# A graph network of 12,500 nodes: the node layers in units of tiles inside the aggregation passes, with two tables and parts kept in DRAM

## The chip, the cores and the metric

The kernel runs on one core of a Trainium2 chip. The metric is device time in microseconds (us) of one execution. The work goes over five engines: PE (matmuls), DVE (vector), ACT (activations), POOL (here mostly the indirect DMAs that gather rows) and SP (plain DMAs).

## The reference

`x` is 12500 × 96, with 200,000 edges `src -> dst`, sorted by `dst`. Six of the seven graph layers are a sum over incoming edges of rows of a node array:

```python
h = relu(layernorm(x)); y = h
for i in range(2):                       # L0
    agg = segment_sum((y @ W0[i] + b0[i])[src], dst)
    y = concat([y @ W1[i] + b1[i], agg]) @ W2[i] + b2[i]
    y = y / std(y)
x = x + y
h = relu(layernorm(x))                   # L1: mean over the edges
x = x + segment_sum(h[src] @ W + b, dst) / max(deg, 1)[:, None]
h = relu(layernorm(x))                   # L2: three GCN layers with self loops
x = x + gcn(relu(gcn(relu(gcn(h))))) 
h = relu(layernorm(x))                   # L3: a small network per edge
e = relu(concat([h[src], h[dst]]) @ Wm1 + bm1) @ Wm2 + bm2
m = segment_sum(e * edge_attr, dst)
out = x + relu(concat([h, m]) @ Wu1 + bu1) @ Wu2 + bu2
```

## The kernel before, in words

Six **passes** (a = 0 to 5; one per sum), then the **edge network** of L3, and between them seven **node phases** (`in`, l0a, l0b, l1, l2a, l2b, l2c) and a last one (`fin`). A node phase turns the sums of a pass (AGG, turned: features on partitions) into the next rows `h`.

**A pass** does its sum in two ways at once. (1) POOL gathers: 88 groups of 8 indirect DMAs (`gather_tile`, L578), each 128 rows of 384 bytes from the DRAM `table` of `h`. PE multiplies them with one-hot matrices that DVE makes (L1167), in `window_sums` (L1522, 8 tiles a group); DVE adds the result to AGG (L1172). (2) Dense blocks: 55 blocks of 128 destinations, for which a count matrix `amat` (fp8, built in pass 0 by POOL's scatters, L593) is multiplied with all of `h` (`piece`, L1598: 100 matmuls of 288 columns a block, in AC = 5 pieces). `h` lies for this in SBUF in three bf16 parts (PARTS: high part, middle part, low part, 3 × 96 columns a tile). The three results of a block are summed (L1240), turned (L1605) and added to AGG (L1251). A pass is 11 **turns** (PE's `turn`, L1607) of 8 slots; a slot is one group of gathers and 5/8 of a block, in an order written out by hand. The flag `fast`, computed from the edges on the chip, chooses this way; else `all_groups` gathers everything.

**A node phase** (`node` on each engine: L1054, L1429, L721, L639) is a stage apart, in 10 chunks of 10 tiles of 125 rows: ACT copies the sums (L735), PE takes the product with the weights (`product`, L1475), DVE runs the chain of layernorm, std or relu (`chunk`, L1066 to L1145), PE turns `h` back to AGG's shape (`turned`, L1486; ACT evicts it, L773), ACT writes the high and middle parts (L762, L781), POOL the two subtractions between them (`split`, L657, L660) and SP stores `h` to `table` (`node_stores`, L390). l0a and l0b also rebuild a turned `h` from the parts (`unsplit`, L1439). `x` is kept in DRAM (`xres`). The next pass begins when all ten chunks are stored: POOL and PE wait for the last of n_st and n_lo:

```python
pool.wait_ge(n_st, 2 + (a + 1) * NCH)      # aggregation(a), POOL
pe.wait_ge(n_lo, 2 + (a + 1) * NCH)        # with_dense(a), PE
```

## Time and profile before

| | before |
|---|---|
| median of 3 runs | 10097.45 us (10087.99 to 10098.42) |
| the profiled execution | 10094.99 us, its span 10093.3 us |
| mean granted PE clock | 0.891 of full |
| PE, POOL busy | 7510.8 us (74%), 6698.0 us (66%) |
| DVE, ACT busy | 2912.4 us (29%), 831.6 us (8%) |

The span is the time between the first and the last instruction of the profiled execution. A share of busy time is an average over stages with different limits, so the stages have to be read one by one. On this time axis the stages are: loads and indices to 265 us, phase `in` to 374, pass 0 to 2434, then l0a, pass 1, l0b, pass 2 and so on; l2c ends at 7923, the edge network at 9885, and `fin` is the rest.

### The profile page before, as it was taken

The page shows a single profiled execution, that of the slowest core. Times are in us where ns is not written, and L with a number is a line of the kernel's source. Part 1 is how long each engine was busy: PE and PEld are TensorE (multiplying, and loading weights), DVE is VectorE, ACT ScalarE, POOL GpSimd, SP SyncE. Part 2 cuts the span into 40 slices and gives each one's busy share as a digit, 9 for nine tenths or more (in the row PEclk, how much of TensorE's full clock was granted, in tenths as well). Part 3 has the DMA queues.
Part 4 walks back from the last instruction along what each step waited for, and adds up shares of the span by engine and source line. Part 5 has one row for each costly group of instructions (what it writes and reads, how often), then busy time and mean ns, then how long its engine had stood idle before and what let it go on. Part 6 is the DMA issues. An engine that isn't in the chain of part 4 may idle for free.

```text
span 10093.3 us, 154577 instructions
## 1 busy us (share of the span) xinstructions
PE 7510.8 (74%) x55633; PEld 6121.5 (61%) x55633; DVE 2912.4 (29%) x5105; ACT 831.6 (8%) x1100; POOL 6698.0 (66%) x6862
## 2 busy tenths in 40 slices
PE   0155554446899869996999799979997677777777
PEld 0144443335777757775777677767776565666665
DVE  1533333331211241113111211121113344444441
ACT  0100000002100120003000200020002111111111
POOL 0577777774677547774777577757773577777771
PEclk9977777777899979996999799979996799999997
DMA  9333333322455435553555355535552344444442
GB/s 372 93 100 96 91 99 99 98 89 60 121 141 142 114 101 142 142 141 105 141 141 142 92 142 141 142 92 141 141 142 85 110 135 136 136 136 135 135 135 65
DMA packets 662964, 1264.24 MB, mean 125 GB/s; under 512 B 238941, under 2 KB 241535, under 8 KB 662757
## 3 DMA queue, kind: packets, MB, share of 16 engines
q1 hardware_dynamic: 409686, 862.57, 28.2%
q0 software_dynamic: 216992, 309.23, 14.2%
q10 hardware_dynamic: 36080, 90.12, 2.3%
q8 instruction: 78, 1.28, 0.1%
q14 instruction: 128, 1.05, 0.0%
HBM read 1112.96 MB, written 148.37 MB: 125 GB/s over the span
## 4 chain that ended last, share of the span: by engine, by line
POOL 61%; issue 21%; PE 7%; DVE 3%; DMA 2%; ACT 2%; SPq 2%; ACTq 0%; DVEq 0%; POOLq 0%
POOL G L578 53%; POOL amat L593 8%; PE PS L1475 2%; SPq L345 2%; PE PS L1598 2%; PE PS L1493 1%; ACT work L735 1%; DMA xres<-work 1%; PE PS L1486 1%; DVE small L1091 1%; PE PS L1439 1%; ACT work L750 0%; PE PS L1454 0%; PE PS L1522 0%; DVE work L1145 0%
## 5 line engine op out<-in xcount | busy, mean ns | idle before, releaser
L578 POOL DMA_INDIRECT G<-table,SRC x5792 | 5531.2, 955 | 1796.8 <-issue 1761.7
L1598 PE MATMUL PS<-PARTS,work 125*128 125x288 bf16 (+1 forms) x33000 | 4313.8, 290 | 729.3 <-DMA work<-amat 729.3
L1598 PEld LDWEIGHTS PS<-PARTS,work 125*128 125x128 fp8e4 x33000 | 3253.6, 99 | 1655.2 <-issue 743.6
L1522 PE MATMUL PS<-work,G 128*96 128x128 f32 (+1 forms) x8448 | 1091.2, 285 | 665.8 <-issue 410.3
L1522 PEld LDWEIGHTS PS<-work,G 128*96 128x96 f32 (+1 forms) x8448 | 1009.8, 172 | 755.4 <-issue 629.0
L1172 DVE TENSOR_TENSOR AGG<-AGG,PS 96x128 f32 (+1 forms) x724 | 206.0, 285 | 3173.5 <-PE PS L1522 2820.3
L593 POOL DMA_INDIRECT amat<-SVAL,ADDR x864 | 847.2, 981 | 274.5 <-issue 260.9
L1167 DVE TENSOR_TENSOR work<-PS,REL 128x1024 f32<-128x1024 f32 x724 | 878.4, 1214 | 49.3 <-POOL PARTS L660 25.1
L1536 PE MATMUL PS<-work,QW 128*96 128x512 f32 x784 | 426.3, 626 | 329.9 <-DMA G<-table,SRC 327.5
L1326 DVE TENSOR_TENSOR work<-work,PS 128x1024 f32<-128x1024 int32 x196 | 393.2, 2006 | 777.4 <-PE PS L1538 770.9
L1475 PE MATMUL PS<-W,work 97*125 97x96 f32 (+1 forms) x1800 | 389.8, 413 | 260.0 <-ACT work L735 129.2
L1233 DVE TENSOR_SCALAR_CACHE_REDUCE work<-work,KEYC 128x384 bf16<-128x384 f32 x864 | 528.2, 611 | 184.9 <-DVE work L1233 115.4
L1240 DVE TENSOR_REDUCE work<-PS 128x96 f32<-128x288 f32 x330 | 151.0, 458 | 1403.0 <-PE PS L1598 1402.9
L1475 PEld LDWEIGHTS PS<-W,work 97*125 97x125 f32 (+1 forms) x1800 | 373.9, 323 | 285.2 <-ACT work L735 139.6
L1538 PEld LDWEIGHTS PS<-ident,G 128*96 128x96 f32 x3136 | 397.8, 168 | 218.2 <-issue 218.2
L1554 PE MATMUL PS<-work 128*96 128x128 f32 x3136 | 383.9, 276 | 195.1 <-DVE work L1177 195.1
L735 ACT ACTIVATE work<-AGG 97x1250 f32 (+1 forms) x60 | 143.7, 2401 | 4476.1 <-DVE AGG L1251 4476.1
L1554 PEld LDWEIGHTS PS<-work 128*96 128x96 f32 x3136 | 347.4, 163 | 221.4 <-issue 221.3
L1538 PE MATMUL PS<-ident,G 128*96 128x128 f32 x3136 | 419.6, 278 | 0.0
L836 ACT ACTIVATE work<-PS,bcols 96x512 f32<-96x512 f32 x392 | 246.5, 677 | 1757.3 <-PE PS L1546 1711.1
L657 POOL TENSOR_TENSOR work<-work,PARTS 125x960 f32<-125x960 f32 x70 | 140.0, 2000 | 373.5 <-ACT PARTS L762 369.0
L1546 PE MATMUL PS<-W,work 97*128 97x96 f32 x3136 | 377.2, 273 | 0.5 <-DVE AGG L1172 0.5
(180 smaller groups left out, 2811.3 us busy)
## 6 DMA issues: line engine op xcount, KB each, us to landing
work<-amat SPq DMA_DIRECT2D x1650, 320.0 KB
work<-in_dst_dram SPq DMA_DIRECT2D x196, 512.0 KB, 5.1
G<-table,SRC POOLq DMA_INDIRECT x5792
amat<-work ACTq DMA_DIRECT2D x55, 1600.0 KB, 17.5
work<-in_edge_attr_dram SPq DMA_DIRECT2D x196, 384.0 KB
work<-keys SPq DMA_DIRECT2D x108, 640.0 KB, 6.3
table<-work SPq DMA_DIRECT2D x70, 468.8 KB
xres<-work SPq DMA_DIRECT2D x30, 468.8 KB
```

The costliest lines, as they stand in the source:

```text
L578: pool.indirect_dma_start(G[:, k, i, 0:D], None, table, bass.IndirectOffsetOnAxis(ap=SRC[:, tile:tile + 1], axis=0)).then_inc(done, 16)
L593: pool.indirect_dma_start(amat, bass.IndirectOffsetOnAxis(ap=ADDR[:, tile:tile + 1], axis=0), SVAL[:, tile:tile + 1], None).then_inc(s_sca ...
L1167: return dve.tensor_tensor(dst, places.unsqueeze(1).to_broadcast([P, TPG, WIN]), rel.unsqueeze(2).to_broadcast([P, TPG, WIN]), ALU.is_equal)
L1233: dve.tensor_scalar(JUNK, KB[k][:, n * P:(n + 3) * P], KEYC[:, bass.ds(tile, 1)], None, ALU.is_equal, ALU.add, accum_out=MULT[:, bass.ds(t ...
L1326: dve.tensor_tensor(OHT[k].rearrange("w (i p) -> w i p", i=TPG), DROW[k].rearrange("w (p i) -> w i p", i=TPG), ESTART[:, bass.ds(g, 1)].un ...
L1475: last = pe.matmul(o, stage[0:rows, j * NP:(j + 1) * NP], w, start=(m == 0), stop=(m == len(parts) - 1))
L1522: last = pe.matmul(PS[0:rows, k, 0:WIN], G[:, place, i, 0:rows], OH[k][:, i, :], start=(i == 0), stop=(i == TPG - 1))
L1536: pe.matmul(PS[0:D, bank, :], QW[:, q, :], OHT[k][:, b * HE:(b + 1) * HE], start=True, stop=False)
L1538: last = pe.matmul(PS[0:D, bank, i * P:(i + 1) * P], G[:, q, 4 * b + i, 0:D], ident[:, :], start=False, stop=(i == 3))
L1546: last = pe.matmul(PS[:, OUT_B[b], (i % 4) * D:(i % 4 + 1) * D], RT[:, i * P:(i + 1) * P], w_m2, start=True, stop=True)
L1554: last = pe.matmul(EWIN, MSG[:, i, :], OH[k][:, i, :], start=(i == 0), stop=(i == TPG - 1))
L1598: last = pe.matmul(PS[:, DENSE_B[b], 0:width], AB[m][0:NP, jj * WIN:(jj + 1) * WIN].bitcast(FP8), PARTS[0:NP, j * PW:j * PW + width], star ...
```

## The change

Nodes are laid out anew: 98 tiles of 128 rows (row = tile × 128 + p; 44 rows of padding) in place of 100 tiles of 125, so a dense block has 98 matmuls, in 7 pieces of 14. The phase after pass a now runs **inside pass a**, on the rows whose sums are complete: in 22 **units**, of 5 tiles (half 0: the dense rows) or 4 tiles (half 1: the gathered rows; the last has 3). Each turn from 1 to 10 carries two units in four steps of one slot each (half 0 from slot 0, half 1 from slot 4; in pass 0 from 2 and 5); the last two units follow the pass.

- The new rows go to the other one of two tables (`tables[k]`); the parts go to DRAM (`newparts`, stored by ACT) and SP loads them into PARTS at the end of the pass (`new_parts`): pieces 0, 1, 2, 4, 5 once the parts of all but the last two units are stored and the dense matmuls are done, pieces 3 and 6 after the last store.
- POOL has no node work left: the two subtractions of the split are DVE's (`rest` L1282, `third_part` L1289). Loads of `x` and stores of table, `x` and parts are issued by ACT.
- Node buffers are single and 5 tiles wide (H, XC, XL, HTS). PE's steps are the first of a slot's end: `product` (L1695) in step 0, `turned` (L1703) in step 2.
- The sum of a block is turned into its own bank (columns 384 to 511), at piece 3 (TURN_AT) instead of piece 1, and the next block in that bank waits for d_add, the add that reads it.
- The degrees are loaded with 12544 runs of 4 bytes (SP, `DEG[:, :]` in the diff), before block 1 of pass 1.
- `in` has 22 units; `fin` has 25 groups of up to 4 tiles, with the turned `h` loaded from DRAM (`hturned`), and buffers of 2.
- `fast` has two more conditions: the base of gather group 108 is at least 6400, and each of the last gathered rows of a turn is at least 7552.

```diff
-NP, NJ = 125, 100
-CH = 10
-PAIRS = NJ // CH // 2
+NT = 98
+NPAD = NT * 128
...
-AC = 5
-ACW = NJ // AC * WIN
+AC = 7
+ACW = NT // AC * WIN
...
+TURN_AT = 3
+HALVES, UNITS = 2, 2 * TURNS
+UNIT_AT = 4
+UT = 5
+SLOT_OF = ((0, UNIT_AT), (2, 5))
+PHASES = ("in", "l0a", "l0b", "l1", "l2a", "l2b", "l2c")
...
-        table = dram("table", (N, D))
+        tables = [dram(f"table{k}", (NPAD, D)) for k in range(2)]
+        hturned = dram("hturned", (D, NPAD))
+        newparts = nc.dram_tensor("newparts", (P, NT * PQ), BF16, kind="Internal").ap()
...
-        table_rows = table.rearrange("(p j) f -> p (j f)", j=NJ)
+        def tiles(half, u):
+            if half == 0:
+                return u * 5, 5, u * 2
+            return u * 4 + DB, 3 if isinstance(u, int) and u == TURNS - 1 else 4, u * 2 + 1
+        def rows_dram(ap, t0, n):
+            return ap[bass.ds(t0 * P, n * P), :].rearrange("(j p) f -> p j f", p=P)
...
+            def new_parts(a):
+                with sp.If(fast > 0):
+                    sp.wait_ge(d_mm, AC + a * DB * AC)
+                    sp.wait_ge(S["par"], prev16(S, "par", a, UNITS - 2))
+                    load_parts(a, (0, 1, 2, 4, 5))
+                    load_block(0, a * DB)
+                    if a < 3:
+                        sp.wait_ge(S["uns"], done(S, "uns", a))
+                    sp.wait_ge(S["par"], 16 * done(S, "par", a))
+                    load_parts(a, (3, 6))
...
+            for a in range(1, 6):
+                if a > 1:
+                    new_parts(a)
+                with sp.If(fast > 0):
+                    with sp.Fori(1, DB) as d:
+                        load_block(d, a * DB)
...
-                def split(c, k):
-                    if name == "fin":
-                        return
-                    parts = parts_of(c)
-                    pool.wait_ge(n_hi, c + (h0 + 1))
-                    pool.wait_ge(n_lo, c + (h0 + 2))
-                    pool.nop(nofuse=True)
-                    pool.tensor_tensor(c3(R1), c3(H[k]), parts[0], ALU.subtract).then_inc(n_r1, 1)
-                    pool.wait_ge(n_mid, c + (h0 + 1))
-                    pool.nop(nofuse=True)
-                    pool.tensor_tensor(parts[2], c3(R1), parts[1], ALU.subtract).then_inc(n_lo, 1)
...
+            def stage(s, phase, half, u):
+                t0, n, v = tiles(half, u)
+                act.wait_ge(s["out"], prev(s, "out", phase, v))
+                act.nop(nofuse=True)
+                act.activation(AGS[phase > 1][:, 0:n * P], AGG[:, bass.ds(t0 * P, n * P)], ACT.Copy).then_inc(s["ags"], 1)
...
+            def step(s, phase, q, half, u):
+                name = PHASES[phase]
+                if name in ("l0a", "l0b") and q == 0:
+                    copy_turned_parts(s, phase, half, u)
+                if q == 0:
+                    stage(s, phase, half, u)
...
+                if name != "l2c" and q == (2 if name == "l0b" else 1):
+                    store_rows(s, phase, half, u)
+                    first_part(s, phase, half, u)
+                if name != "l2c" and q == (3 if name == "l0b" else 2):
+                    second_part(s, phase, half, u)
+                if name in ("l1", "l2a", "l2b") and q == 2 or name == "l2c" and q == 1:
+                    evict(phase, half, u)
+                if name != "l2c" and q == (2 if name == "l0a" else 3):
+                    store_parts(s, phase, half, u)
...
+                if q == 3:
+                    next_x(phase, half, u)
...
+                            if start or not 0 <= q < 4:
+                                continue
+                            if q == 0 and half == 0:
+                                act.wait_ge(d_add, i * SIDE + (a * DB + 1))
+                            if q == 0 and half == 1:
+                                act.wait_ge(f_acc, i * SLOTS + (a * GG + UNIT_AT + 2))
+                            step(S, a + 1, q, half, i - 1)
...
+            def rest(s, phase, half, u):
+                t0, size, v = tiles(half, u)
+                dve.wait_ge(s["hi"], this(s, "hi", phase, v))
+                dve.tensor_tensor(u3(SQ if phase else RIN, size), u3(H, size), parts_of(phase, t0, size)[0],
+                                  ALU.subtract).then_inc(s["r1"], 1)
+            def third_part(s, phase, half, u):
+                t0, size, v = tiles(half, u)
+                parts = parts_of(phase, t0, size)
+                dve.wait_ge(s["mid"], this(s, "mid", phase, v))
+                dve.tensor_tensor(parts[2], u3(SQ if phase else RIN, size), parts[1], ALU.subtract).then_inc(s["lo"], 1)
...
-                def add_block(d, windows):
-                    block_cols = AGG[0:rows, bass.ds(d * WIN, WIN)]
-                    dve.wait_ge(d_turn, d + (b0 + 1))
-                    dve.wait_ge(f_acc, windows + (g0 + 2))
-                    dve.wait_ge(d_add, d + (b0 + 1))
-                    dve.tensor_tensor(block_cols, block_cols, PS[0:rows, 4, 0:WIN], ALU.add).then_inc(d_add, 1)
+                def add_block(d, b, windows):
+                    block_cols = AGG[0:rows, bass.ds(d * WIN, WIN)]
+                    dve.wait_ge(d_turn, d + (b0 + 1))
+                    dve.wait_ge(f_acc, windows + (g0 + 2))
+                    dve.wait_ge(d_add, d + (b0 + 1))
+                    dve.tensor_tensor(block_cols, block_cols, PS[0:rows, DENSE_B[b], 3 * P:4 * P], ALU.add).then_inc(d_add, 1)
...
+            def product(s, phase, half, u):
+                name = PHASES[phase]
+                t0, n, v = tiles(half, u)
+                sums = lambda j, rows: AGS[phase > 1][0:rows, j * P:(j + 1) * P]
+                if name in ("l0a", "l0b"):
+                    pe.wait_ge(s["hts"], this(s, "hts", phase, v))
...
+                for j in range(n):
+                    o = PS[:, 6, j * D:(j + 1) * D]
+                    if name in ("l0a", "l0b"):
+                        l = name == "l0b"
+                        pe.matmul(o, HTS[:, j * P:(j + 1) * P], w_self[l], start=True, stop=False)
+                        last = pe.matmul(o, sums(j, D + 1), w_nb[l], start=False, stop=True)
+                    elif name == "l1":
+                        last = pe.matmul(o, sums(j, D + 1), w_l1, start=True, stop=True)
+                    else:
+                        last = pe.matmul(o, sums(j, D), w_l2[("l2a", "l2b", "l2c").index(name)], start=True, stop=True)
+                last.then_inc(s["out"], 1)
...
+            def step(s, phase, q, after, half, u):
+                name = PHASES[phase]
+                if q == 0 and not after and name in ("l0a", "l0b"):
+                    unsplit(s, phase, half, u)
+                if q == 0 and after:
+                    product(s, phase, half, u)
+                if after and (q == 2 and name in ("l1", "l2a", "l2b") or q == 1 and name == "l2c"):
+                    turned(phase, half, u)
+                if after and q == 2 and name == "l2c":
+                    halves(half, u)
...
-                        pe.wait_ge(d_cp, d + (b0 - 1))
+                        pe.wait_ge(d_add, d + b0)
+                    if not first and isinstance(d, int) and d == 0:
+                        pe.wait_ge(p_ld[m], 16 * a)
...
-                def turn_sums(d, b):
-                    pe.wait_ge(d_cp, d + (b0 + 1))
-                    pe.wait_ge(d_add, d + (b0 + 1))
-                    pe.transpose(PS[0:rows, 4, 0:WIN], DSB[DENSE_T[b]][:, 0:rows], ident[:, :]).then_inc(d_turn, 1)
+                def turn_sums(d, b):
+                    pe.wait_ge(d_cp, d + (b0 + 1))
+                    pe.transpose(PS[0:rows, DENSE_B[b], 3 * P:4 * P], DSB[DENSE_T[b]][:, 0:rows], ident[:, :]).then_inc(d_turn, 1)
...
+                def turn(i, start=False):
+                    from_b = -off if start else 0
+                    for s in range(SLOTS):
+                        for half in range(HALVES):
+                            if not start and s == SLOT_OF[first][half]:
+                                step(S, a + 1, 0, False, half, i - 1)
+                        if first:
+                            gathered(i, s)
+                        for q in SHARE[s]:
+                            b, m = divmod(q, AC)
+                            d = i * SIDE + (b + off)
+                            if b < from_b:
+                                continue
+                            if m == TURN_AT and not (start and b == from_b):
+                                turn_sums(d - 1, (b - 1) % SIDE)
+                            piece(d, b, m)
+                        if not first:
+                            gathered(i, s)
+                        for half in range(HALVES):
+                            q = s - SLOT_OF[first][half]
+                            if start or not 0 <= q < 4:
+                                continue
+                            step(S, a + 1, q, True, half, i - 1)
...
```

**Place 1, PE, one turn of pass 3.** Before, in phase l2a, apart from the pass (L1475 the product, L1486 the turned `h`):

```order
L1475 MATMUL PS<-W,work 125x96 [waits n_read,n_ags]
L1475 MATMUL PS<-W,work 125x96 x9
L1481 REGISTER_ALU
L1482 REGISTER_ALU [waits n_h]
L1486 MATMUL PS<-ident,work 96x125 [waits n_ev]
L1486 MATMUL PS<-ident,work 96x125 x9
```

Now, in a turn of pass 3 (L1825 the dense pieces, L1831 the turned block sum, L1745 the sums of the gathered rows, L1695 the product of a unit of 5 tiles):

```order
L1831 MATMUL PS<-ident,work 96x128 [waits d_cp]
L1825 MATMUL PS<-PARTS,work 128x288 [waits d_ld3]
L1825 MATMUL PS<-PARTS,work 128x288 x13
L1810 ISA
L1811 ISA [waits f_oh]
L1745 MATMUL PS<-work,G 96x128 [waits f_acc,f_rows0]
L1745 MATMUL PS<-work,G 96x128 x7
L1681 ISA
L1682 REGISTER_ALU [waits n_read]
L1685 REGISTER_ALU [waits n_ev]
L1695 MATMUL PS<-W,work 128x96 [waits n_ags]
L1695 MATMUL PS<-W,work 128x96 x4
L1825 MATMUL PS<-PARTS,work 128x288 [waits d_ld4]
L1825 MATMUL PS<-PARTS,work 128x288 x13
```

The product of ten tiles stood between others of its kind; it is now one of five tiles between a window's sums and a dense piece, and everything behind it on PE stands if n_read, n_ev or n_ags comes late.

**Place 2, DVE, slot 1 of a turn of pass 3** (L1357 a one-hot, L1251 to L1274 the chain of the unit, L1439 the add of a block, L1362 the add of a window):

```order
L1251 TENSOR_TENSOR work<-PS,DINV 128x480
L1255 TENSOR_TENSOR work<-work,W 128x480 [waits n_read]
L1196 REGISTER_ALU
L1218 ISA [waits n_chain]
L1220 REGISTER_ALU [waits n_tab]
L1223 REGISTER_ALU [waits n_r1,n_hi]
L1274 SCALAR_TENSOR_TENSOR work<-work,DINV 128x480 [waits n_tr]
L1439 ISA [waits d_add,f_acc,d_turn]
L1439 TENSOR_TENSOR AGG<-AGG,PS 96x128
L356 ISA
L356 TENSOR_LOAD rowi
L1385 REGISTER_ALU
L1388 REGISTER_ALU [waits f_acc,f_sum]
```

The three instructions of 480 columns stood in the stage apart, ten times with 960 columns; L1439, the add whose d_add PE's next block in that bank waits for, stands right behind them.

**Place 3, PE, the end of a pass (l2a):** the two units that are left, of 5 and 3 tiles.

```order
L1695 MATMUL PS<-W,work 128x96 [waits n_ags,n_ev,n_read]
L1695 MATMUL PS<-W,work 128x96 x4
L1703 MATMUL PS<-ident,work 96x128 [waits n_read,n_h]
L1703 MATMUL PS<-ident,work 96x128 x4
L1695 MATMUL PS<-W,work 128x96 [waits n_ags,n_ev,n_read]
L1695 MATMUL PS<-W,work 128x96 x2
L1703 MATMUL PS<-ident,work 96x128 [waits n_read,n_h]
L1703 MATMUL PS<-ident,work 96x128 x2
```

Before, ten products and ten turned chunks stood here.

## Rows read from the trace of the kernel before

**Rows 1.** The page, the chain of work that ended last, by engine

```profile
POOL 61%; issue 21%; PE 7%; DVE 3%; DMA 2%; ACT 2%; SPq 2%; ACTq 0%; DVEq 0%; POOLq 0%
```

**Rows 2.** Windows: span, PE, PEld, DVE, ACT, POOL busy (x), PE clock, DMA, GB/s

```profile
265.00:374.00 109.00, 0.00 (x0) 0.00 (x0) 54.37 (x63) 41.99 (x47) 46.58 (x30) 1.00 0.32 88
374.00:2434.00 2060.00, 1033.64 (x6963) 804.27 (x6963) 700.51 (x2070) 22.54 (x108) 1538.75 (x1568) 0.75 0.31 95
...
3475.00:3700.00 225.00, 121.08 (x722) 116.81 (x723) 122.31 (x133) 102.25 (x110) 50.69 (x37) 0.55 0.24 73
...
4742.00:5633.00 891.00, 853.14 (x6963) 694.79 (x6963) 163.47 (x285) 0.00 (x0) 669.54 (x704) 0.99 0.53 140
5633.00:5745.00 112.00, 65.18 (x300) 60.43 (x300) 36.41 (x32) 62.69 (x59) 36.82 (x19) 0.56 0.13 42
...
7647.00:7923.00 276.00, 154.93 (x700) 145.66 (x700) 107.33 (x112) 91.95 (x90) 44.32 (x30) 0.51 0.22 70
7923.00:9885.00 1962.00, 1455.36 (x10057) 1177.27 (x10058) 846.59 (x971) 243.97 (x388) 1485.76 (x1562) 0.98 0.49 136
9885.00:10093.00 208.00, 165.85 (x756) 110.22 (x756) 18.69 (x21) 31.71 (x64) 11.08 (x16) 0.73 0.18 50
4850.00:5550.00 700.00, 672.57 (x5508) 548.18 (x5506) 128.20 (x224) 0.00 (x0) 530.27 (x558) 1.00 0.54 141
```

**Rows 3.** Groups by line, pass 3 (4742 to 5633 us): busy, mean ns, idle before

```profile
L1598 PE MATMUL PS<-PARTS,work 125*128 125x288 bf16 x5500 | 701.0, 286 | 13.0 <-DMA work<-amat 13.0
L578 POOL DMA_INDIRECT G<-table,SRC x704 | 669.5, 951 | 218.4 <-issue 214.2 <-SPq L394 4.1
```

**Rows 4.** PE's waits, inside pass 3 (4850 to 5550 us): total, times, longest

```profile
PE PS L1522 <- issue: 19.9, 26, 1.7
```

**Rows 5.** Timeline at the start of pass 3, POOL: start, us

```profile
4742.84 1.00 POOL L578 DMA_INDIRECT G<-table,SRC  x1 [4.15 <-SPq L394]
```

**Rows 6.** Timeline, end of pass 3 and the stage l2a

```profile
5625.66 0.95 POOL L578 DMA_INDIRECT G<-table,SRC  x1 [0.30 <-issue]
...
5633.10 0.28 DVE L1251 TENSOR_TENSOR AGG<-AGG,PS 96x128 f32<-96x128 f32 x1
...
5636.16 8.71 PE L1475 MATMUL PS<-W,work 96*125 96x96 f32 x40 [3.45 <-ACT work L735]
...
5642.38 1.16 DVE L1133 TENSOR_TENSOR work<-work,W 125x960 f32<-125x960 f32 x1
...
5646.47 2.92 POOL L657 TENSOR_TENSOR work<-work,PARTS 125x960 f32<-125x960 f32 x1 [19.86 <-ACT PARTS L762]
...
5647.86 2.54 DVE L1145 SCALAR_TENSOR_TENSOR work<-work,DINV 125x960 f32<-125x960 f32 x1 [0.28 <-DVE work L1133]
```

**Rows 7.** Groups by line, 3475 to 3700 us (phase l0b)

```profile
L1475 PE MATMUL PS<-W,work 97*125 97x96 f32 x400 | 85.9, 415 | 68.3 <-ACT work L802 68.3
L1439 PE MATMUL PS<-identb,PARTS 125*96 125x125 bf16 x300 | 32.0, 293 | 1.4 <-DVE AGG L1251 1.4
```

**Rows 8.** The chain, ends of phases l0a and l2c: start, us, what

```profile
2577.67 6.00 DMA table<-work
...
7909.03 13.70 DMA xres<-work
```

**Rows 9.** The chain, near the end of pass 1

```profile
3437.34 3.38 DMA G<-table,SRC
```

**Rows 10.** All gathers of a stretch of pass 0: ns min/median/max, first and last start

```profile
L578 POOL DMA_INDIRECT G<-table,SRC x629: 977/982/991, 499.8 to 2297.5; - x158
```

**Rows 11.** The same in the edge network

```profile
L578 POOL DMA_INDIRECT G<-table,SRC x1434: 947/952/968, 8000.2 to 9799.9; - x180
```

**Rows 12.** Timeline of the start, SP: the edges' sources, in runs of 32 bytes

```profile
1.39 13.68 SPq L345 DMA_DIRECT2D SRC<-in_src_dram  x1
```

**Rows 13.** Timeline of `fin`, PE: matmuls of 500 columns

```profile
9932.29 1.08 PE L1452 MATMUL PS<-work,W 96*96 96x500 f32 x2 [1.42 <-ACT work L802]
...
9934.95 1.02 PE L1452 MATMUL PS<-work,W 96*96 96x500 f32 x2
```

1190 lines of the change are left out of this document (656 added, 534 removed).

## The prediction

> **What bounds the kernel now.** I read the chain of waits first: POOL and its "issue" gaps hold 82% of it [rows 1]. That is a mean over stages, so the windows come next [rows 2]. They show two kinds. Inside pass 3 (891 us) POOL and PE are both nearly full, PE at 853 us busy with the granted clock at 0.99 (the 2.4 GHz level). In the stage l2a (112 us) no engine is full and the clock is 0.56, about the 1.2 GHz level; l0b takes 225 us and l2c 276, and none of them issues a gather of a pass. Five passes with the four stages between them take 7647 − 2434 = 5213 us.
>
> What sets a pass? Its first gather starts at 4742.84 [rows 5], the last at 5625.66, and the last add ends at 5633.38 [rows 6]: 890.5 us, of which 703 steps of (5625.66 − 4742.84) / 703 = 1.256 us and a tail of 7.7. A turn of 64 gathers is then 80.35 us. PE is busy 672.57 of 700 us inside the pass [rows 2], so it needs 77.2 us a turn, and 19.9 us of its idle time is a wait at L1522 that the profile puts to nothing, the sums of gathered rows [rows 4]. **So POOL leads, but PE has only 3.1 us a turn in reserve.** This is what the change runs into.
>
> **The change, part by part.**
>
> *The stages vanish, up to two units.* 20 of 22 units go beside the pass. What stays is: end of pass to first gather (I call it B), and end of pass to the last reloaded piece of parts (U). For l2a I work it out: copy of 5 tiles 1.0; product 10 entries at 4.51/20 = 0.22 each at the low clock (that entry price is 85.9/400 in [rows 7]) 2.2; DVE three steps of 480 columns, each half of 1.16 and a little [rows 6], 2.0, with handovers `h` at 6; subtractions on DVE, the second unit behind them, its `h` at about 14; store landing 3.5. B is 18. For the landing the trace has 3.4 us for 128 rows of 384 bytes [rows 9] and 6.0 for a store of 480 KB [rows 8]; the unit's store is 3 × 128 rows, so I take the first. U adds the two later parts, their store and their load, 2.5 + 3.5 + 4: 25. The longer chains (layernorm, std, `unsplit`), scaled by the lengths of the stages before (150, 225, 159, 112 us [rows 2] for those shown): B = 28, 42, 27, 18, U = 34, 47, 33, 25 for l0a, l0b, l1, l2a (and l2b).
>
> *PE gets the node work.* Dense: 10 matmuls fewer a turn (98 for 100 in 5 blocks), 701.0/5500 = 0.127 each [rows 3], 77.2 − 1.2 = 76.0, so 836 for 11 turns. Node work of a turn's 9 tiles, at the full clock half of 0.22, i.e. 0.113 an entry: product 18 entries 2.0, turned 9 entries 1.0, register work 0.6: 3.7 for l1, l2a, l2b; l0b has 36 entries 4.1, 27 bf16 transposes (0.107 each at the low clock [rows 7], 0.08 taken) 2.2 and 0.6: 6.9; l2c with its products of halves 8.2. PE is in order, so each unit also has the time in which it stands for ACT or DVE. The trace has no such row inside a pass. Its nearest waits are those of PE for ACT or DVE in a stage, 3.45 us for the first product [rows 6], 1.42 in `fin` [rows 13]; the steps stand a slot (10 us) apart so the most of it is hidden: I take 1.0 us a unit, 20 a pass, bounds 0 and 50.
>
> *Sum of the passes.* Period = the larger of POOL's path, B + 890.5, and PE's, U − 5 + 836 + ten turns of node work + 20 (−5: the last reload serves pieces 3 and 6, and PE has three pieces of work before it).
> - pass 1 (l0b inside): POOL 918.5; PE 34 − 5 + 836 + 69 + 20 and 9 for the degrees: 963
> - pass 2 (l1): 932.5; 47 − 5 + 836 + 37 + 20 = 935
> - pass 3 (l2a): 917.5; 33 − 5 + 893 = 921
> - pass 4 (l2b): 908.5; 25 − 5 + 893 = 913
> - pass 5 (l2c): 908.5; 25 − 5 + 836 + 82 + 20 = 958
>
> 4690 against 5214: **−524**. POOL and PE are within a few us of each other in passes 2 to 4. The 9 for the degrees: 24960 runs of 32 bytes took 13.68 us to move [rows 12]; 12544 runs at that rate are 7 and 2 to land, while block 1 queues behind on SP; bounds 0 (prefetched blocks) and 14.
>
> *l2c to the edge network* was 7647 to 7923, 276.7 us to the first gather. Now two units, whose chain includes the halves, and a store of `x` that took 13.70 us as ten tiles [rows 8]: 40. **−237**.
>
> *Pass 0* gains l0a's two units a turn. POOL is busy 1538.75 of 2060 and PE and DVE a half or less [rows 2]; that hides them. I take +8 (0 to 24) for waits in front of one-hots. *Phase in* was 109 us; 22 units at 5.4 is 117, set-up 5 less: +3. Together **+11**.
>
> *fin*: 208 us for 10 chunks [rows 2]; now 25 groups with buffers of 2. Period of a group: the hidden layer 1.7, the last layer 0.9 (from one record of 500 columns to the next there are 2.66 us [rows 13], which I read as three matmuls of 0.89; the hidden layer has two), DVE and the issue of the store 1.1 (384 columns, by half of 1.16 [rows 6], and two issues), and what a load adds when two buffers do not hide it, 2.6 of 3.4 [rows 9]: 6.3 at the full clock, 8.9 at the low one; the clock there was 0.73, so 8.3. 24 + 25 × 8.3 = 232 from 208: **+23**.
>
> Costed at nothing: ACT's and SP's extra DMA issues (ACT was busy 0.00 in pass 3 [rows 2]; if its queue backs up, the parts' store is late next); DVE's two subtractions (163 us busy of 891 there; if they are late, d_add holds PE's next block); the later turn (TURN_AT), with 1.7 us of matmuls for each piece in between. The parts' and table's stores beside the pass add about 15 MB to a stretch that moved 140 GB/s.
>
> Sum: −524 − 237 + 11 + 23 = −727. Against the profiled execution's span of 10093.3: 9366. The run itself was 1.7 above its span and the median 2.5 above the run: **9370**.
>
> The trace's stores of `h` are 480 KB in long runs, 6.0 us [rows 8]; the new ones have rows of 384 bytes, and the gathers of such rows landed in 3.4 [rows 9]. The Trainium skill ("DMA: Bandwidth & Descriptors", Specifications) speaks against them: the line rate needs transfers of at least 512 bytes, and below that the engines read, modify and write. No row here shows a store of that kind; at double the landing the page would give 3.5 us more at each of B and U, about 20 us in all, and the forecast would be near 9390.
>
> **The rivals.**
>
> *DVE holds up POOL.* When POOL had its own subtractions in the stage, one instruction of DVE took 2.54 us in place of 1.16 while one of POOL took 2.92 [rows 6]: operations with both operands in SBUF exclude each other. If gathers are excluded too, each such DVE step delays POOL by about 0.6. Per unit: 2 in l0a, 5 in l0b and l1, 4 in l2a to l2c, so 2.4, 6.0 and 4.8 a turn. +24 in pass 0; POOL's path of passes 1 to 4 goes to 978, 992, 965, 956, which is 16, 57, 44 and 43 above the sum, in pass 5 nothing. 9554. For it: gathers of pass 0, beside a busy DVE, took a median of 982 ns, against 952 in the edge network [rows 10, 11]. Against: in that edge network too DVE is busy 847 of 1962 us [rows 2]. The Trainium skill ("SBUF — State Buffer", Who interferes with whom) limits it to GpSimd instructions that read SBUF; a gather reads its indices there, and whether that counts no row tells, since DVE's steps in the edge network have one operand in PSUM. Chance 0.15.
>
> *PE stands longer.* ACT and DVE serve a unit in order behind one-hots, window adds and evictions, each of 0.3 to 1.2 us, and a late n_h lets PE stand at L1703 with all the dense pieces behind it. At 2.5 us a unit, 1.5 more over 100 units: 9520. For: single buffers, and a product that waits n_read of the unit before. Against: a slot lies between the steps. Chance 0.13.
>
> *Slower: no overlap at all.* The whole chain of a unit is waited out by PE inside the pass. Then the stages come back in another place: 10093 + 11 + 23, the reload of parts at 15 in each of five passes and 9: 10211. It decides from some 6.5 us of standing a unit on (727 over 110 units). Against: the wait stands a slot behind the step. Also here: `fast` comes out false; all gathers, six passes of 1568 × 1.256, about 16000. The limits of its two new conditions depend only on sorted random edges (gather group 108 starts at edge 108 × 1024 of 200,000, so near node 6912, above 6400), so below 0.01. Both 0.04.
>
> *Cheaper*: handovers hidden, −100: 9270. Chance 0.06.
>
> **How the numbers follow.** My forecast has 0.62, 9310 to 9440 by the bounds of its unknown costs (handovers −100, landings and degrees +40 and the like). The range 9250 to 9600 takes in the port, the PE and the cheap case, and leaves out 0.04 and the tails. Faster by over 0.2% (about what a measurement can tell here: 20 us) is all but the no-overlap case: 0.95; within 0.2% 0.01; slower 0.04.
>
> **What would show it.** Gathers back to back at 1.256 across a pass (else the port case); pass periods of 963, 935, 921, 913, 958 from last add to last add; PE near 97% busy in passes 1 and 5; B of 18 to 42 us and 40 at l2c; `fin` near 235. PE waits at L1695 and L1703 above 2 us a unit mean the second rival. The forecast is wrong if a unit's chain takes more than its four slots, or if the table's stores land after 10 us or more.

## The result, and the profile after

| | before | after |
|---|---|---|
| median, 4 runs each | 10097.94 us | **9342.4 us** (9333.29 to 9354.19) |
| ratio | | 0.9254, 95% interval 0.9238 to 0.9270 |
| span of the profiled execution | 10093.3 us | 9331.5 us |

Forecast: 9370, range 9250 to 9600. The stages of the changed kernel (windows: span, PE, PEld, DVE, ACT, POOL busy, granted PE clock, DMA share, GB/s); the short ones are the gaps from the last add of a pass to the next first gather, the long ones begin with a gather and end with the last add:

```profile
353.50:2403.00 2049.50, 1077.87 (x7490) 852.43 (x7491) 770.77 (x2210) 98.18 (x257) 1536.16 (x1566) 0.76 0.32 100
2403.00:2427.80 24.80, 11.49 (x72) 9.18 (x70) 9.22 (x18) 7.08 (x15) 0.00 (x0) 0.59 0.79 307
2427.80:3326.50 898.70, 879.19 (x7467) 743.59 (x7465) 306.60 (x589) 93.99 (x191) 675.59 (x704) 1.00 0.57 160
...
4298.20:5196.30 898.10, 861.92 (x7110) 720.69 (x7108) 217.67 (x386) 47.47 (x90) 676.31 (x704) 0.99 0.53 150
5196.30:5221.50 25.20, 10.22 (x53) 7.48 (x54) 7.94 (x12) 4.37 (x9) 0.04 (x1) 0.59 0.84 321
5221.50:6117.50 896.00, 859.16 (x7096) 717.46 (x7094) 216.20 (x384) 47.44 (x90) 675.58 (x704) 0.99 0.54 150
6117.50:6142.90 25.40, 10.22 (x52) 7.49 (x53) 7.94 (x13) 4.37 (x9) 0.00 (x0) 0.60 0.88 327
6142.90:7080.50 937.60, 897.37 (x7457) 758.86 (x7455) 275.03 (x504) 58.02 (x110) 675.68 (x704) 0.99 0.54 155
7080.50:7122.90 42.40, 13.62 (x56) 11.81 (x56) 11.86 (x26) 5.40 (x11) 0.04 (x1) 0.54 0.23 61
7122.90:9090.60 1967.70, 1456.78 (x10099) 1178.84 (x10100) 849.38 (x973) 245.48 (x390) 1490.19 (x1567) 0.99 0.46 135
9090.60:9331.50 240.90, 139.06 (x391) 80.13 (x389) 17.87 (x33) 18.13 (x27) 0.95 (x1) 0.56 0.23 62
```

They answer to [rows 2]. The stages of 112 to 276 us are gone; in their place are gaps of 25 to 42 us, with the DMA engines 0.62 to 0.88 busy in the five gaps between passes and 0.23 in the one behind l2c. Inside passes 1 to 4 PE is busy 859 to 879 of some 898 us and in pass 5 897 of 938, POOL as before (676 to 680 for 670).

| part | before | forecast | after |
|---|---|---|---|
| start to first gather | 387.9 | 391 | 353.8 |
| first gather to last add, pass 0 | 2045 | 2053 | 2049 |
| pass 1 with its gap | 1042 | 963 | 924 |
| pass 2 | 1108 | 935 | 938 |
| pass 3 | 1051 | 921 | 932 |
| pass 4 | 1007 | 913 | 921 |
| pass 5 | 1006 | 958 | 963 |
| l2c, to the edge network's first gather | 277 | 40 | 42 |
| last gather to the end (fin) | 202 | 225 | 241 |

The passes sum to 4678 (forecast 4690, before 5214). The edge network itself takes 1968 us in both.

How a boundary looks now, l2a, from the chain of waits (start, us, what):

```profile
5196.70 0.75 ACT work L737
...
5197.59 1.34 PE PS L1695 x10
...
5200.33 0.67 DVE work L1274
...
5201.02 13.85 DMA table<-work
...
5214.96 0.47 DVE work L1274
...
5215.45 5.18 DMA table<-work
...
5221.46 0.95 POOL G L631
```

The last add ends at 5196.3, `h` of the first unit (5 tiles) is there 4.7 us later, and then the table's store of 240 KB takes **13.85 us** to land. H is a single buffer: DVE's next L1274 waits for that landing, then the store of the last unit (3 tiles, 144 KB) takes 5.18. The gap behind pass 4 looks the same, with 14.04 and 5.24. In the gap of 33.6 us behind pass 2 the long landing is that of a store to `xres`, 12.91.

Waits of PE inside passes 3 (4400 to 5100 us), 1 (2600 to 3200) and 5 (6250 to 7040), in that order (us in total, times, longest):

```profile
PE PS L1745 <- DMA G<-table,SRC: 13.5, 9, 1.9
PE PS L1745 <- issue: 10.5, 12, 1.3
...
PE PS L1745 <- DMA G<-table,SRC: 4.6, 5, 1.6
...
PE PS L1695 <- ACT work L737: 25.5, 18, 2.0
```

In passes 1 to 4 the list has no wait of PE for ACT or DVE. In pass 5 it has one, 25.5 us in 18 waits at a unit's product. There the gathers too wait for PE, which they do in no other of these passes (POOL's waits, 2427 to 7080 us, all of them in pass 5):

```profile
POOL G L631 <- PE PS L1745: 17.7, 16, 2.3
```

And the final layers, from the chain:

```profile
9188.26 2.67 DMA work<-hturned
9190.98 2.02 PE PS L1934 x2
...
9197.78 2.61 DMA work<-hturned
9200.51 2.02 PE PS L1934 x2
```

One group of 4 tiles every 9.6 us, and each begins with a load of `hturned` (2.6 us) that starts only after the output of two groups earlier.

Last, the gathers. Most take 0.95 us, as before [rows 3], but some do not (timeline of pass 3):

```profile
4547.31 0.95 POOL L631 DMA_INDIRECT G<-table,SRC  x1 [0.30 <-issue]
...
4548.55 0.54 DVE L1289 TENSOR_TENSOR work<-work 128x384 bf16<-128x384 f32 x1
4548.57 1.35 POOL L631 DMA_INDIRECT G<-table,SRC  x1 [0.30 <-issue]
```

This gather starts 0.02 us after L1289, a DVE subtraction with both operands in SBUF, and takes 1.35 us. Of the 3520 gathers of passes 1 to 5, 137 take over 1.0 us (1.00 to 1.45), about 27 a pass. All 137 start inside a DVE operation with both operands in SBUF, and all of them end 0.82 to 0.84 us after that operation's end; of the 3331 gathers that start at any other moment none takes over 1.0 us. So such a gather is held until the DVE operation is over, less the 0.13 us or so that it needs before it comes to the held part. (Of the other 52 that start inside one, 38 start in its last 0.18 us, and 14 within 0.05 us of its start; these 52 are not longer.) In sum it is 35 us over the five passes for 484 such operations of 292 us, an eighth of their length, and the mean step of the gathers is 1.2645 us in passes 1 and 4, where it was 1.2560.

### The profile page after: what moved, and what is told of

Read it like the earlier page. It is cut to its first block, busy times and chain, and to the rows that moved or that the text cites. A ratio compares the mean times of both kernels' runs of the same rounds, so it can differ in the third digit from the quotient of the medians.

```text
span 9331.5 us, 158512 instructions
## 1 busy us (share of the span) xinstructions
PE 7113.4 (76%) x54589; PEld 5836.1 (63%) x54589; DVE 3107.8 (33%) x5997; ACT 753.9 (8%) x1453; POOL 6427.3 (69%) x6672
## 3 DMA queue, kind: packets, MB, share of 16 engines
q1 hardware_dynamic: 548120, 849.57, 29.2%
## 4 chain that ended last, share of the span: by engine, by line
POOL 59%; issue 21%; PE 12%; DMA 3%; ACTq 3%; DVE 2%; ACT 1%; SPq 0%; DVEq 0%; POOLq 0%
POOL G L631 51%; POOL amat L646 8%; PE PS L1825 7%; ACTq L718 2%; PE PS L1745 2%; DMA xres<-work 1%; DMA work<-hturned 1%; DMA table<-work 1%; PE PS L1934 1%; PE PS L1712 1%; PE PS L1935 0%; PE PS L1943 0%; PE PS L1695 0%; DMA amat<-SVAL,ADDR 0%; DMA work<-keys 0%
## 5 line engine op out<-in xcount | busy, mean ns | idle before, releaser
L1825 PE MATMUL PS<-PARTS,work 128*128 128x288 bf16 (+1 forms) x32340 | 4216.2, 291 | 641.3 <-DMA work<-amat 617.2
L1825 PEld LDWEIGHTS PS<-PARTS,work 128*128 128x128 fp8e4 x32340 | 3213.2, 100 | 1503.2 <-issue 657.0
L1745 PE MATMUL PS<-work,G 128*96 128x128 f32 (+1 forms) x8448 | 1099.7, 287 | 621.5 <-DMA G<-table,SRC 314.8
L1745 PEld LDWEIGHTS PS<-work,G 128*96 128x96 f32 (+1 forms) x8448 | 1024.4, 173 | 676.6 <-issue 505.1
L1362 DVE TENSOR_TENSOR AGG<-AGG,PS 96x128 f32 (+1 forms) x724 | 205.8, 284 | 2723.3 <-PE PS L1745 2370.3
L1357 DVE TENSOR_TENSOR work<-PS,REL 128x1024 f32<-128x1024 f32 x724 | 878.6, 1214 | 1.3 <-issue 1.3
L1761 PEld LDWEIGHTS PS<-ident,G 128*96 128x96 f32 x3136 | 394.2, 166 | 215.8 <-issue 215.8
L1761 PE MATMUL PS<-ident,G 128*96 128x128 f32 x3136 | 415.7, 277 | 0.0
L1769 PEld LDWEIGHTS PS<-W,work 97*128 97x128 f32 x3136 | 365.6, 192 | 0.7 <-DVE AGG L1362 0.7
L1759 PEld LDWEIGHTS PS<-work,QW 128*96 128x96 f32 x784 | 104.0, 166 | 359.2 <-issue 184.7
L1439 DVE TENSOR_TENSOR AGG<-AGG,PS 96x128 f32 (+3 forms) x330 | 92.8, 281 | 701.3 <-PE PS L1831 699.8
L737 ACT ACTIVATE work<-AGG 97x640 f32 (+4 forms) x132 | 89.1, 675 | 1658.6 <-DVE AGG L1439 778.2
```

The costliest lines, as they stand in the source:

```text
L1357: return dve.tensor_tensor(dst, places.unsqueeze(1).to_broadcast([P, TPG, WIN]), rel.unsqueeze(2).to_broadcast([P, TPG, WIN]), ALU.is_equal)
L1745: last = pe.matmul(PS[0:rows, k, 0:WIN], G[:, place, i, 0:rows], OH[k][:, i, :], start=(i == 0), stop=(i == TPG - 1))
L1759: pe.matmul(PS[0:D, bank, :], QW[:, q, :], OHT[k][:, b * HE:(b + 1) * HE], start=True, stop=False)
L1761: last = pe.matmul(PS[0:D, bank, i * P:(i + 1) * P], G[:, q, 4 * b + i, 0:D], ident[:, :], start=False, stop=(i == 3))
L1769: last = pe.matmul(PS[:, OUT_B[b], (i % 4) * D:(i % 4 + 1) * D], RT[:, i * P:(i + 1) * P], w_m2, start=True, stop=True)
L1825: last = pe.matmul(PS[:, DENSE_B[b], 0:width], AB[m][:, jj * WIN:(jj + 1) * WIN].bitcast(FP8), PARTS[:, j * stride:j * stride + width], st ...
```

## Experiments

The first four ran on one chip together, the next four on another; before took 10096.99 and 10106.77 us there. From run to run a pass that an experiment leaves alone stays within 5 us (passes 3 and 4: 928 to 932 and 921 to 924 us), pass 5 within 14 (963 to 977), so the later experiments are read by passes and not by the whole.

**1. The load in `fin`.**

```diff
+            def next_turned(f, k):
+                sp.wait_ge(z_hid, f + 1)
+                n = 4 if not isinstance(f, int) or f + 2 < NT // 4 else NT % 4
+                sp.dma_start(HT[k][:, 0:n * P], hturned[:, bass.ds((f + 2) * (4 * P), n * P)]).then_inc(z_ht[k], 16)
...
+                    next_turned(f, k)
                     out_rows(f, k)
-                    turned_rows(f + 2, k)
+                    next_x_rows(f + 2, k)
```

> One edit to the changed kernel, in fin alone: SP loads the turned h of group f+2 as soon as the hidden layer of group f is done, before it waits for the output of group f. Theory A: fin is one serial chain in the changed kernel (load 2.6, hidden layer 3.7, last layer 1.9, add, store issue, next load), 9.6 us a group for 25 groups; with the load out of the chain PE sets it, about 6 us at the low clock, so the time from the last gather to the end falls from 241 us to about 150 and the whole from 9342 to about 9250. Theory B: PE at the low clock bounds fin already; nothing changes, 9342.

Measured: 9244.73 us (ratio to before 0.9155, interval 0.914 to 0.917), 98 below the changed kernel. From the last gather to the end 133.3 us in place of 240.9, so 108 less; pass 5, which the edit leaves alone, took 7 us more in this run. Theory A holds. The windows row of `fin` in this run:

```profile
9099.20:9232.50 133.30, 116.50 (x389) 69.62 (x388) 17.88 (x33) 18.10 (x27) 0.92 (x1) 0.70 0.42 112
```

and its timeline, from one group's hidden layer to the next:

```profile
9165.70 1.92 PE L1945 MATMUL PS<-work,W 96*96 96x512 f32 x2
...
9168.43 0.33 SPq L572 DMA_DIRECT2D work<-hturned  x1
...
9171.03 2.02 PE L1945 MATMUL PS<-work,W 96*96 96x512 f32 x2
...
9171.92 0.40 SPq L581 DMA_DIRECT2D out_dram<-MULT  x1
```

The load (L572) is issued 2.7 us behind the start of a hidden layer and no longer behind the output (L581) of the same group. A group now takes 5.2 us. PE's wait for `hturned` fell from 96 to 10 us in sum, and with the clock granted at 0.70 in place of 0.56 its matmuls of `fin` took 116.5 us in place of 139.1; that second part is why it gave more than the 90 expected.

**2. The load of x in l2c.**

```diff
                 if q == 0:
                     stage(s, phase, half, u)
+                if name == "l2c" and q == 0:
+                    load_x(phase, half, u)
...
                 if PHASES[phase] not in ("l0b", "l1", "l2c"):
                     return
+                if PHASES[phase] == "l2c":
+                    return
...
-                if PHASES[a + 1] in ("l0b", "l1", "l2c"):
+                if PHASES[a + 1] in ("l0b", "l1"):
                     load_x(a + 1, 0, 0, first=a == 1)
```

> One edit, in pass 5: ACT loads the next x of l2c behind its copy of the next unit's sums, no longer ahead of it (where it stands until the xres store has landed). Theory A: pass 5 is bound by PE, and the 25.5 us for which PE waits at the product for ACT's copy are on its path: pass 5 from last add to last add falls from 963 to about 938, the whole by 25. Theory B: the waits are hidden behind POOL's gathers; pass 5 stays 963.

Measured: 9298.98 us (0.9207, 0.9192 to 0.9222), 43 below the changed kernel. Pass 5 takes 930 us in place of 963 (expected 938), its gap to the edge network 39 in place of 42: 36 us, and the rest of the 43 lies in stages that the edit leaves alone. The wait at the product is gone from the list of PE's waits, POOL's wait for PE fell from 17.7 to 1.8 us, and what is left of the pass is 896 us of PE in 910:

```profile
6132.00:7042.00 910.00, 895.97 (x7484) 760.87 (x7483) 277.09 (x508) 59.28 (x113) 675.89 (x704) 0.99 0.60 161
```

Theory A holds: pass 5 was set by PE, and ACT, standing for the landing of a store, held PE up. Even so the last add comes 15.6 us after the last gather, where it is 7 to 10 in the other passes: PE still ends last in pass 5.

**3. Parts reloaded behind the table stores.**

```diff
                     sp.wait_ge(S["par"], prev16(S, "par", a, UNITS - 2))
+                    sp.wait_ge(S["tab"], 16 * done(S, "tab", a))
                     load_parts(a, (0, 1, 2, 4, 5))
```

> One edit, at the end of each pass: SP loads the first five pieces of the parts only after the last table stores have landed. Theory A (contention): the table's store took 13.9 us because the reload of 5 MB and the first block are moved at the same time at some 410 GB/s; alone it lands in about 4, and the gap to the first gather falls from 25 to about 16 us in passes 2 to 5; PE starts about as before; the whole falls by 20 to 40. Theory B (stores of rows of 384 bytes are slow by themselves): the store still takes 14 us, the gap stays 25 and PE starts some 15 us later; the whole grows by 40 to 60.

Measured: 9339.3 us (0.9248, 0.9233 to 0.9264), 3 less than the changed kernel, within its scatter. The mechanism of theory A is there, its saving is not. The same boundary, in the chain of waits of this run:

```profile
5201.02 3.52 DMA table<-work
```

and in its timeline:

```profile
5205.38 0.95 POOL L632 DMA_INDIRECT G<-table,SRC  x1 [23.28 <-DMA table<-work]
...
5221.99 3.28 PE L1826 MATMUL PS<-PARTS,work 128*128 128x288 bf16 x13 [20.06 <-DMA work<-amat]
```

These 3.52 us are the store of the last unit, 144 KB, which took 5.18 in the changed kernel. The 240 KB store of the unit ahead of it is no longer on the chain: its 640 packets of 384 bytes are all moved 2.0 us after it is issued (5193.55 to 5195.56), where in the changed kernel they were spread over 9.8 us (5204.69 to 5214.46) and the landing took 13.85. The gap is 17.0 us in place of 25.2. So the 13.85 us were the reload's traffic, not the rows of 384 bytes. But PE's first dense matmul waits 20 us for `amat`, which now lies behind five pieces of parts: it starts 34 us after the last add in place of 20, where it was expected about as before. Passes 3 and 4 still gain 12 and 9 us, pass 2 gains 4, and pass 1 loses 7; pass 5 took 971, within the 963 to 977 of the runs that leave it alone.

The run also tells what sets passes 1 and 2. PE's first dense matmul starts 21 and 25 us later in them (42.0 and 54.3 us after the last add for 21.2 and 29.2). Pass 2 does not grow, pass 1 only by 7, and its last add then comes 16.9 us after its last gather in place of 9.8: PE had some 14 us to spare in pass 1, and about 25 in pass 2.

**4. No overlap: all 22 units behind the pass.** (ACT, DVE and PE: `step(...)` taken out of `turn`, `nodes(S, a + 1)` behind it.)

> The units are not taken beside the pass: all 22 of a phase follow it, in a loop, everything else as in the changed kernel. Theory A (the gain is the overlap): at the pass's end a unit took 8 to 16 us, so 20 more of them in six phases cost 1000 to 1900 us, less what the passes give back (a step of 1.256 us instead of 1.265, pass 5 no longer bound by PE, together about 75): 10300 to 11100. Theory B (the gain comes from the new layout, the two tables and the reloaded parts, and the overlap is paid back by slower gathers and matmuls): near 9342 or up to 9700.

Measured: 11019.88 us, one run. The gaps to the next first gather are 302, 431, 322, 214 and 214 us, and 480 at l2c; before they were 151, 216, 160, 116, 116 and 277. So theory A: the new units in a row take 1.7 to 2.0 times as long as the old chunks of ten tiles, and beside the pass they cost nearly nothing. In this run every gather step of passes 1 to 5 is 1.256 us, and no gather takes over 1.0: what lengthens gathers are the units' operations.

**5 and 6. Four more DVE operations a unit, with two SBUF operands, and with one.**

```diff
+                if phase in (4, 5):
+                    dve.wait_ge(s["r1"], this(s, "r1", phase, v))
+                    for n in range(4):
+                        dve.tensor_tensor(u3(XC, size), u3(SQ, size), u3(H, size), ALU.max).then_inc(exs, 1)
...
+                        dve.reduce_sum(EXJ[:, 0:size], u3(H, size), AX).then_inc(exs, 1)
```

> Passes 3 and 4 only: four more DVE operations a unit, each with both operands in SBUF (480 or 384 columns, written to a buffer that nothing reads there). Theory A (DVE and POOL share a read port, and a gather reads its indices through it for a short time): the four such operations a unit of the changed kernel made some 20 gathers a pass up to 0.5 us longer, 5 to 7 us a pass; with eight it is about twice that, so passes 3 and 4 grow by some 6 us each. Theory B (the gathers are longer because DVE or the DMA queues are busier in general): the same growth as with the control, which reads one operand. Theory C (the price of my rival, each such operation holds POOL for all its length): 50 us a pass.

> The control: passes 3 and 4 only, four more DVE operations a unit of the same length, a sum over one SBUF operand. Theory A: no gather is longer for it, passes 3 and 4 stay at 932 and 921 within the 4 us that they differ between runs. Theory B: as much growth as in x5_two.

Measured: 9370.03 and 9346.73 us, one run each. Passes 3 and 4 took 936.5 and 928.1 us with two operands, 930.9 and 920.5 with one (changed kernel: 931.7 and 921.2). The gathers of pass 3 with two operands (groups by line: busy us, mean ns):

```profile
L633 POOL DMA_INDIRECT G<-table,SRC x696 | 674.4, 969 | 212.2 <-issue 212.2
```

and with one:

```profile
L633 POOL DMA_INDIRECT G<-table,SRC x700 | 672.2, 960 | 213.3 <-issue 213.3
```

Theory A, in its size too: 9 ns on each of 704 gathers are 6.3 us a pass. The 88 added operations of 0.66 or 0.56 us come to 53 us and cost about as much as the 88 that were there; as many with one operand cost nothing. The single gathers say it without any mean: in passes 3 and 4, of 73 that start inside an added operation with two operands 43 take over 1.0 us (up to 1.42), of 79 that start inside an added one with one operand none does (longest 0.955). Two gathers of that run were held in the same way though they started 0.02 and 0.05 us before such an operation and not inside it. The Trainium skill says so ("SBUF — State Buffer", Who interferes with whom: such an instruction "contends with a GpSimd instruction that reads SBUF"). These runs add that an indirect gather is one, and that it costs about an eighth of the operations' length.

**7. PE given more.** l2a's and l2b's products are computed three times into the same place (`for _ in range(3)`).

> Passes 3 and 4 only: each product of l2a and l2b is computed three times into the same place, 36 more matmul records a turn, 0.12 us each: 4.2 us of PE a turn. By my forecast's terms (76.0 dense and sums, 3.7 node work, 2.0 handovers in a turn of 80.35) PE has nothing left and each pass grows by 42 us. If the trace is right (PE idle 24 us in 700, so 2.8 us a turn, and no wait for ACT or DVE), each grows by about 14 us; if PE's idle time is larger than the records show, by nothing.

Measured: 9372.1 us, one run. Passes 3 and 4 grew by 4.7 and 8.7 us, not by 42, and less than 14. PE was busy 897 of 904 us in pass 4, for 859 of 895. With them the last add comes 14 and 16 us after the last gather in place of 8 and 7, so PE now ends last. PE's reserve in the changed kernel is then 4.2 less 0.5 to 0.9, about 3.5 us a turn; by my terms it was below zero.

**8. The split given back to POOL** in passes 3 and 4 (`rest` and `third_part` of phases 4 and 5 in POOL's order, three groups later).

> Passes 3 and 4 only: the two subtractions of the split are given back to POOL, between its gathers, three groups later than DVE had them. Theory A (POOL sets the pass): 4 subtractions a turn at about 0.9 us (1.94 for 960 columns before) and 0.3 to issue, 4.8 us a turn, so each pass grows by about 50 us, and the gathers get back the 2 to 3 us that DVE's two subtractions cost them. Theory B (PE sets the pass): the passes stay at 932 and 921.

Measured: 9438.23 us, one run. Passes 3 and 4 take 973.8 and 959.4, that is 42 and 38 more (expected 50). POOL's rows of pass 3:

```profile
L631 POOL DMA_INDIRECT G<-table,SRC x704 | 675.0, 959 | 249.3 <-issue 207.2 <-DMA table<-work 40.6 <-ACT work L803 1.2
L675 POOL TENSOR_TENSOR work<-work 128x480 f32<-128x480 f32 x10 | 11.1, 1109 | 0.2
L677 POOL TENSOR_TENSOR work<-work 128x480 bf16<-128x480 f32 x10 | 11.0, 1104 | 0.2
L675 POOL TENSOR_TENSOR work<-work 128x384 f32<-128x384 f32 x9 | 8.3, 924 | 0.2
L677 POOL TENSOR_TENSOR work<-work 128x384 bf16<-128x384 f32 x9 | 8.3, 923 | 0.2
```

The 38 subtractions are 11.1 + 11.0 + 8.3 + 8.3 = 38.7 us of POOL. From the first gather to the last, pass 3 takes 33 us more (922.3 for 889.6), and in it POOL waits for nothing but 1.2 us of ACT: that part is POOL's queue, with 7 us less of "issue" than in the changed kernel. The other 9 us stand behind the last gather (17.1 us to the last add for 8.5), since the subtractions come later and ACT's copy stands behind them in ACT's order (L765 waits 116.5 us for POOL's L677): PE waits 46.1 us for that copy in 15 waits, and ends last. Pass 4 shows the same, 34 and 9, and a gap 5 us shorter. So the stretch of gathers is as long as POOL's queue; that the sum came out as 42 and 38 for 38.7 is partly chance. Without the move of the split to DVE the overlap would have given back about 40 us in each of these passes.

**9 to 12. Two further versions, on other chips.** In x10 the first block's counts are loaded ahead of the wait of experiment 3; x12 is that with experiments 1 and 2.

```diff
-                    load_parts(a, (0, 1, 2, 4, 5))
                     load_block(0, a * DB)
+                    sp.wait_ge(S["tab"], 16 * done(S, "tab", a))
+                    load_parts(a, (0, 1, 2, 4, 5))
```

> As x8_late (the parts are reloaded only behind the last table stores), but the first dense block's counts are loaded ahead of that wait, not behind five pieces of parts. In x8_late the gap to the first gather fell to 17 us in passes 4 and 5, but PE's first dense matmul came at 34 us in place of 20, since its counts lay behind 5 MB. Expected: gap to the first gather 17 to 20 us, first dense matmul at 22 to 26, each of passes 2 to 4 about 9 us shorter than in the changed kernel, passes 1 and 5 within 5 of it; the whole 9300 to 9320. If the first matmul stays at 34, the parts themselves are what it waits for, and the whole stays at 9340.

> The three edits together: the turned h of fin prefetched (-98 alone), the load of x behind the copy in l2c (-43 alone), the counts first and the parts behind the table stores (-20 to -40 alone). They lie in different stages, and pass 5, no longer bound by PE, can use the shorter gap: 9160 to 9190. If the parts' order takes back in pass 5 what the second edit gave, 9200 to 9220.

> The kernel of x10_block_first again: that run met a chip on which the kernel before took 11731 us in place of 10097, with dense matmuls slower for all kernels, so that PE set every pass. On a chip where before takes about 10097: gap to the first gather 17 us in passes 4 and 5 (both chips' gaps are DMA and ACT work), first dense matmul at about 21, passes 3 and 4 some 9 us shorter than in the changed kernel; the whole 9295 to 9320.

> The kernel of x12_best again, for the same reason. On a chip where before takes about 10097: 9150 to 9190; pass 5 at 920 to 930, fin at about 133, the gap to the edge network 39.

Both pairs met chips on which the kernel before took 11731.2 and 11732.03 us. Measured: 11366.03 and 11357.18 us for the first version (ratios 0.968 and 0.9684), 11247.32 and 11245.06 for the second (0.9584 and 0.9587, interval 0.9573 to 0.9600). The changed kernel itself did not run there, so these ratios do not say how the versions stand to it. Two things can be read. Between the two versions lie 119 and 112 us, and nearly all of it is `fin` (265 to 158 us from the last gather to the end); pass 5 took 1221 and 1214 us in the first version and 1229 twice in the second, so the second edit gave nothing there. And the gap of pass 4 is 17 us with the first dense matmul at 21 to 22, as expected: with the counts first, both come early. Whether that makes passes 2 to 4 shorter, and whether the whole falls to 9150 to 9190 on the first chip, stays open: no run shows it.

## Why the prediction was right

**What vanishes: right.** The stages go and gaps of 25 to 42 us stay; experiment 4 shows that the overlap is all of it, 1680 us against the same units in a row. Without it the changed kernel is 920 us slower than the one before.

**Which engine sets a pass: partly wrong.** I had PE ahead of POOL in all five. It is POOL in passes 3 and 4 (experiments 7 and 8) and in passes 1 and 2 (experiment 3, where PE could start 21 and 25 us later for 7 and 0 us), and PE in pass 5 (experiment 2). Three terms of PE's path were too large. Node work: PE was busy 862 us in pass 3 against 839 for dense and sums (853.1 [rows 2] less 14 for 110 matmuls), 2.3 us a turn for a forecast of 3.7, of which 0.6 was register work that busy time does not count; in pass 1 4.0 for 6.9. Handovers: 1.0 us a unit in the forecast, 0 in passes 1 to 4, and 25.5 us in pass 5, where it was ACT's wait for a store. The degrees: 9 us in the forecast; PE's waits at dense matmuls come to 3.4 us in the first 170 us of pass 1. In pass 1 PE also began its dense matmuls 8 us sooner than forecast (21.2 us after the last add for 29). With that PE's path was below POOL's, and pass 1 forecast 39 us too long (963 for 924).

**The gap B: the mechanism of the landing was wrong.** I took 3.5 us for the table's store, from a quiet queue, and B = 27 us for l1 and 18 for l2a and l2b. The store met the reload of the parts and took 13.85; B was 33.6, 25.2 and 25.4. My own sign of being wrong, "if the table's stores land after 10 us or more", came true at the ends of passes 3 and 4. That and 6 us of longer gathers made passes 3 and 4 11 and 8 us too short. I had priced the reload for PE, and rightly (first dense matmul at 20 us in passes 4 and 5, as forecast), but not for POOL, which waits for another transfer on the same engines. These errors and those of PE's path had opposite signs, so the sum of the passes came within 12 us: luck in part. The whole is no better. In spans it is 9331.5 for a forecast of 9366, and the parts differ by −37 (the start), −4 (pass 0), −12 (the passes, of which pass 1 alone is −39 and the others +27), +2 (the gap of l2c) and +16 (`fin`).

**fin: right in kind.** A load behind each group was forecast as 2.6 us and measured as 2.6; I missed the hidden layer's second half and the issue times of the chain, 9.6 us for 8.3: +39 for +23. The 8.3 was not sound either: 6.3 at the full clock and 8.9 at the low one give 7.3 to 7.7 at 0.73. And the clock was not the 0.73 of before but 0.56. **The start: wrong.** 34 us earlier, for +3. The layernorm's first square is at 251.6 us, where it stood at 276.6, behind a load of x that was issued only at 269: 25 us. The other 9 are phase `in` itself, 102 us from that square to the first gather for 111, since two units take 7.9 us together and not the 10.8 that I took. The traces tell this, no run tested it.

**The rivals.** DVE against POOL exists, at about an eighth of the price that I gave it (6 to 10 us a pass for 48 to 60). I charged the whole length of each operation to POOL. The hold does last to the operation's end, but it meets only a gather that starts inside the operation, 137 of 3520, and then for what is left of it. The 982 ns of pass 0 that I held for this rival are no sign of it: all of those gathers are alike (977 to 991 [rows 10]), and they are as long in experiment 4, which has no units there; why they are longer stays open. PE standing longer: only in pass 5, 1.3 us a unit. Small stores: the Trainium skill ("DMA: Bandwidth & Descriptors", Specifications) has transfers under 512 bytes read, modified and written, below the line rate. The 3.5 us more that I had put beside it do not show here: with the reload held back a store in rows of 384 bytes landed in 3.52 us, as forecast without it. Its rate may well be lower (240 KB in 1.1 us are some 225 GB/s, where the reload has 403), but at this size that is half a microsecond.

## What to carry to other kernels

When the serial work of a stage is moved beside a loop, find which engine's queue the loop is, and give it none of the work, not even small pieces: what went on DVE, ACT and PE cost about 1% of the pass, and 39 us of it on POOL made a pass 42 and 38 us longer. A reload at a stage's end delays the small store that the next stage waits for; held back behind it, it delays what lies behind the reload, so the first consumer's data go ahead of both. That both then come early was measured, that the whole gets faster was not. Look in each in-order queue for a wait on a store's landing that stands in front of a copy for the bounding engine; moving one such issue behind the copy took 36 us out of pass 5 and its gap, and moving one load ahead of the wait for an output took 108 out of `fin`. On the chips where PE was slower the first gave nothing and the second gave the same.

## What the runs showed of the hardware

A DVE operation with two SBUF operands holds an indirect gather that starts within it until it is over: the gather ends 0.82 to 0.84 us after the operation, up to 0.5 us late (1.00 to 1.45 us for 0.95). With one SBUF operand it does not. A 240 KB store in 384-byte rows was moved within 2.0 us of its issue with nothing else under way, and landed in 13.85 us beside a reload, when 5.6 MB went in 14 us (403 GB/s). And chips differ: on two of them the kernel before took 11731 and 11732 us. In x12b_best the granted PE clock was 0.93 in pass 4 and 0.82 in the edge network, where the changed kernel on its chip has 0.99 in both (windows of that run):

```profile
6389.00:7535.00 1146.00, 960.32 (x7144) 758.05 (x7144) 221.07 (x390) 50.53 (x96) 675.00 (x701) 0.93 0.45 123
8803.00:11097.00 2294.00, 1736.64 (x10040) 1440.85 (x10040) 838.80 (x964) 243.04 (x387) 1482.66 (x1560) 0.82 0.41 115
```

DVE's and POOL's operations lasted as long as on the other chips (a one-hot 1213 ns, a gather 964). In pass 4 POOL waited 204.7 us for PE's L1761, where it waited for PE in none of passes 1 to 4 on the first chip, and in passes 1 and 5 it was 244.5 and 301.4, so PE set these passes; the gather steps, 1.57 to 1.67 us in all five, say the same of the other two. At the full clock PE was no slower there: dense matmuls follow each other at 123 ns on both chips. But in pass 4 the clock stood at the low level for 149 of the 1146 us, in 27 stretches, where on the first chip it was 14 of 896 in two, and in the edge network for 834 us, where it was 53. That is a part of it only: PE was busy 960 us for 859, and idle for 186 where it had been 37, most of it with no wait that the profile shows. Why these chips grant less, and where that idle time comes from, stays open.
